# Graph attention block: how W1 and W2 are weighed, and where the preparation of W2 and W3 stands in the queues

## The reference

```python
h = relu(layernorm(x))
xl = (h @ W1).reshape(B, N, 4, 128)              # W1: 256 x 512
e = leaky_relu(sum(xl * att_src1)[:, :, None] + sum(xl * att_dst1)[:, None], 0.2)
h1 = elu(softmax(masked(e), axis=1) applied to xl + b1)
xl2 = h1 @ W2                                    # W2: 512 x 256, one head
e2 = the same with att_src2, att_dst2
x = x + (softmax(masked(e2)) applied to xl2 + b2)
h2 = relu(layernorm(x))
x = x + h2 + h2 @ (weights[0] + weights[1]).T + sum of bias rows by label
```

## Time and profile before

| | |
|---|---|
| median of 3 runs | 498.49 us (498.0 to 501.19) |
| profiled execution, its own time | 501.3 us |
| its span | 499.5 us |
| busy: PE, DVE, ACT, POOL | 471.8, 428.5, 399.6, 320.2 us |
| mean granted tensor clock | 0.988 |
| a pair of x from issue to landing, median of 32 | 2.8 us |

### The profile page before, as it was taken

How to read it: one execution, slowest core, us unless ns; L and a number is a source line. 1 busy time by engine, 2 the same in 40 slices (tenths; PEclk the granted TensorE clock), 3 DMA queues, 4 the chain that set the end, 5 groups by cost and what they waited for, 6 DMA issues and landing times. The chain is left out here.

```text
span 499.5 us, 15008 instructions
## 1 busy us (share of the span) xinstructions
PE 471.8 (94%) x3428; PEld 424.6 (85%) x3428; DVE 428.5 (86%) x1885; ACT 399.6 (80%) x1476; POOL 320.2 (64%) x492
## 2 busy tenths in 40 slices
PE   4488999999999999999999999999999999999875
PEld 1367899999999999999999999999999999999853
DVE  7977888888888988898888988898888988888654
ACT  3247988889888988888888988888888888888831
POOL 2435767676666667766766667766766676766631
PEclk9989999999999999999999999999999999999996
DMA  8011111111111111111111111110111111000001
GB/s 233 21 33 34 36 49 39 56 55 43 36 54 54 54 33 53 54 54 30 46 54 54 54 33 53 54 54 27 48 54 54 54 33 53 22 23 25 21 23 42
DMA packets 29146, 23.70 MB, mean 47 GB/s; under 512 B 1976, under 2 KB 28860, under 8 KB 29120
## 3 DMA queue, kind: packets, MB, share of 16 engines
q1 hardware_dynamic: 27328, 21.44, 14.0%
q10 hardware_dynamic: 1792, 1.98, 1.4%
HBM read 14.56 MB, written 8.39 MB: 46 GB/s over the span
## 5 line engine op out<-in xcount | busy, mean ns | idle before, releaser
L444 ACT ACTIVATE L<-L,nmax 128x128 f32<-128x128 f32 x256 | 99.1, 391 | 5.4 <-DVE nmax L746 3.9
L331 POOL TENSOR_TENSOR h_lo<-h,h_hi 128x512 fp32r<-128x512 f32 x64 | 82.0, 1282 | 24.4 <-DVE h2n L704 20.2
L347 POOL TENSOR_TENSOR P<-L,rsum 128x512 f32<-128x512 f32 x64 | 66.6, 1041 | 20.0 <-DVE rsum L752 18.6
L932 PE MATMUL pY<-w_hi,h_hi 128*128 128x258 f32 x256 | 76.3, 298 | 1.4 <-POOL h_lo L331 1.4
L933 PE MATMUL pY<-w_lo,h_hi 128*128 128x258 f32 x256 | 72.7, 284 | 0.0
L934 PE MATMUL pY<-w_hi,h_lo 128*128 128x258 f32 x256 | 72.3, 282 | 0.0
L460 ACT ACTIVATE elu_e<-pA,minus_ones 128x512 f32<-128x512 f32 x64 | 44.0, 688 | 32.0 <-PE pA L920 32.0
L920 PE MATMUL pA<-PT,xl 128*128 128x128 f32 x512 | 67.7, 276 | 0.5 <-ACT PT L452 0.5
L758 DVE SCALAR_TENSOR_TENSOR h<-elu_e,pA 128x512 f32<-128x512 f32 x64 | 44.0, 688 | 22.8 <-ACT elu_e L460 20.0
L920 PEld LDWEIGHTS pA<-PT,xl 128*128 128x128 f32 x512 | 62.2, 192 | 0.7 <-ACT PT L452 0.7
L746 DVE CUSTOM_DVE_ANT_0 L<-pZ,L 128x128 f32<-128x128 f32 x256 | 58.7, 286 | 3.0 <-ACT L L439 2.9
(11 more groups left out here) (154 smaller groups left out, 1584.2 us busy)
## 6 DMA issues: line engine op xcount, KB each, us to landing
x_all<-in_x SPq DMA_DIRECT2D x32, 256.0 KB, 2.8
out<-x_all SPq DMA_DIRECT2D x32, 256.0 KB, 2.2
adj_all<-in_adj SPq DMA_DIRECT2D x32, 128.0 KB, 2.6
x_all<-in_L_gnn_W ACTq DMA_DIRECT2D x2, 512.0 KB, 6.3
rhs<-lhs SPq DMA_DIRECT2D x64, 6.0 KB
rhs<-lhs SPq DMA_DIRECT2D x64, 1.0 KB
x_all<-in_L_gnn_weights ACTq DMA_DIRECT2D x2, 256.0 KB, 7.3
x_all<-in_L_gnn_att_src ACTq DMA_DIRECT2D x1, 128.0 KB, 6.3
```

The source lines that it names most:

```text
L331: pool.tensor_tensor(h1_lo[p][:, :, :].rearrange("p a b -> p (a b)"), h1[p][:, :], h1_hi[p][:, :, :].rearrange("p a b -> p (a b)").bitcast ...
L347: pool.tensor_tensor(P1[p][:, :, :], L1[p][:, :, :], rsum1[p][:, :].unsqueeze(2).broadcast_to([128, H, 128]), ALU.mult).then_inc(s_P1, 1)
L444: last = act.activation(L1[p][:, h, :], L1[p][:, h, :], ACT.Exp, bias=nmax1[p][:, h:h + 1], scale=-1.0, accum_out=sum1[p][:, h:h + 1])
L932: pe.matmul(pY[:, 0:C2], h1_hi[p][:, k, :], w2_hi[:, k, :], start=(k == 0), stop=False)
```

## The change

The multiplication and the reduction are replaced by one fused operation for each sum (eight over 128 elements for a vector of W1, four over 256 for a vector of W2), each with its accumulator read. `weigh_w2_src` moves from slot -1 to slot 0, behind `leaky1`; `weigh_w2_dst` stays in slot 0 but moves behind `layer_norm1` and `residual1`; `sum_w3` moves from slot 0 to slot 1, behind `take_off_excess`; `split_w3` and tensor's `transpose_w3` move to slots 3 and 2. The sync queue issues the second pair of x and adj only when W1 has landed.

```diff
@@ load
                 if after(g, 4):
                     sp.wait_ge(s_n0, g - 2)
                     sp.wait_ge(s_bn1, g - 2)
+                elif g:
+
+                    sp.wait_ge(s_w1dma, 16)
@@ vector
+            def weigh(rows, vector, products, sums, width):
+
+                blocks = vector.shape[1] // width
+                for k in range(rows.shape[1]):
+                    for b in range(blocks):
+                        cols, m = slice(b * width, (b + 1) * width), k * blocks + b
+                        last = dve.tensor_tensor_reduce(products[:, m * width:(m + 1) * width], rows[:, k, cols], vector[:, cols],
+                                                        1.0, 0.0, ALU.mult, ALU.add, sums[:, m:m + 1])
+                return last
@@ weigh_w1_src
-                link(dve.tensor_tensor(w1_att[:, 0, :].rearrange("p (k n) -> p k n", k=KD), w1_f[:, :, :],
-                                       pA[:, :].unsqueeze(1).broadcast_to([128, KD, HF]), ALU.mult))
-                dve.tensor_reduce(w1_scores[:, 0, :], w1_att[:, 0, :].rearrange("p (m f) -> p m f", f=FH), AX.X, ALU.add)
+                weigh(w1_f, pA[:, :], w1_att[:, 0, :], w1_scores[:, 0, :], FH)
@@ weigh_w1_dst
+                link(weigh(w1_f, pZ[:, :], w1_att[:, 1, :], w1_scores[:, 1, :], FH))
@@ weigh_w2_src
+                weigh(w2_f, att2_bc[:, 0, :], w2_att[:, 0, :], w2_scores[:, 0, :], D)
@@ weigh_w2_dst
+                link(weigh(w2_f, att2_bc[:, 1, :], w2_att[:, 1, :], w2_scores[:, 1, :], D))
@@ the vector list
-            (features1, 1), (sum_w3, 0), (recip1, 1), ... (weigh_w2_dst, 0), (count1, 0), ... (stats1, -4), (weigh_w2_src, -1), (weigh_w1_src, -2), ... (leaky1, 0), (release2, 4), (layer_norm1, -2), (residual1, 4), (label_terms, 3), (take_off_excess, 1), (split_w3, 0), (low_h2, 5), ...
+            (features1, 1), (recip1, 1), ... (count1, 0), ... (stats1, -4), (weigh_w1_src, -2), ... (leaky1, 0), (weigh_w2_src, 0), (release2, 4), (layer_norm1, -2), (residual1, 4), (weigh_w2_dst, 0), (label_terms, 3), (take_off_excess, 1), (sum_w3, 1), (split_w3, 3), (low_h2, 5), ...
@@ the tensor list
-            ... (transpose_h, -1), (transpose_w3, 0), (attend1, 2), ...
+            ... (transpose_h, -1), (transpose_w3, 2), (attend1, 2), ...
```

More of the change, by code:

```diff
@@ L572, in weigh_w1_dst @@
                 dve.wait_ge(s_spread, 2)
-                link(dve.tensor_tensor(w1_att[:, 1, :].rearrange("p (k n) -> p k n", k=KD), w1_f[:, :, :],
-                                       pZ[:, :].unsqueeze(1).broadcast_to([128, KD, HF]), ALU.mult))
-                link(dve.tensor_reduce(w1_scores[:, 1, :], w1_att[:, 1, :].rearrange("p (m f) -> p m f", f=FH), AX.X, ALU.add))
+                link(weigh(w1_f, pZ[:, :], w1_att[:, 1, :], w1_scores[:, 1, :], FH))
                 cols = w1_scores[:, :, :].rearrange("p j (k h) -> p k j h", k=KD)
@@ L589, in weigh_w2_src @@
                 dve.wait_ge(s_w2dma, 64)
-                link(dve.tensor_tensor(w2_att[:, 0, :].rearrange("p (k n) -> p k n", k=KH), w2_f[:, :, :],
-                                       att2_bc[:, 0, :].unsqueeze(1).broadcast_to([128, KH, D]), ALU.mult))
-                dve.tensor_reduce(w2_scores[:, 0, :], w2_att[:, 0, :].rearrange("p (k n) -> p k n", k=KH), AX.X, ALU.add)
+                weigh(w2_f, att2_bc[:, 0, :], w2_att[:, 0, :], w2_scores[:, 0, :], D)
             def weigh_w2_dst(g, p):
@@ L596, in weigh_w2_dst @@
                     return
-                link(dve.tensor_tensor(w2_att[:, 1, :].rearrange("p (k n) -> p k n", k=KH), w2_f[:, :, :],
-                                       att2_bc[:, 1, :].unsqueeze(1).broadcast_to([128, KH, D]), ALU.mult))
-                link(dve.tensor_reduce(w2_scores[:, 1, :], w2_att[:, 1, :].rearrange("p (k n) -> p k n", k=KH), AX.X, ALU.add))
+                link(weigh(w2_f, att2_bc[:, 1, :], w2_att[:, 1, :], w2_scores[:, 1, :], D))
                 scores = w2_scores[:, :, :].rearrange("p j k -> p k j")
@@ L806, in residual2 @@
                 dve.tensor_tensor(of_graph(x_all, g, D), pF[:, 0:D], of_graph(x_all, g, D), ALU.add).then_inc(s_out, 1)
-            pipeline(dve, [(features1, 1), (sum_w3, 0), (recip1, 1), (low_h, -1), (largest_labels, 6), (largest_of_rows, 6), (weigh_w2_dst, 0), (count1, 0), (count2, 3), (elu_max, 2), (recip2, 4), (stats1, -4), (weigh_w2_src, -1), (weigh_w1_src, -2), (layer_norm2, 5), (release1, -4), (low_rows1, -1), (aggregate1, -4), (residual2, 6), (leaky1, 0), (release2, 4), (layer_norm1, -2), (residual1, 4), (label_terms, 3), (take_off_excess, 1), (split_w3, 0), (low_h2, 5), (stats2, 4), (leaky2, 3), (aggregate2, 4), (high_scores2, 2), (weigh_w1_dst, -2), (zero_counts, 2), (low_scores2, 2), (largest_label, 9)])
+            pipeline(dve, [(features1, 1), (recip1, 1), (low_h, -1), (largest_labels, 6), (largest_of_rows, 6), (count1, 0), (count2, 3), (elu_max, 2), (recip2, 4), (stats1, -4), (weigh_w1_src, -2), (layer_norm2, 5), (release1, -4), (low_rows1, -1), (aggregate1, -4), (residual2, 6), (leaky1, 0), (weigh_w2_src, 0), (release2, 4), (layer_norm1, -2), (residual1, 4), (weigh_w2_dst, 0), (label_terms, 3), (take_off_excess, 1), (sum_w3, 1), (split_w3, 3), (low_h2, 5), (stats2, 4), (leaky2, 3), (aggregate2, 4), (high_scores2, 2), (weigh_w1_dst, -2), (zero_counts, 2), (low_scores2, 2), (largest_label, 9)])
             dve.wait_ge(s_label, 1)
@@ L986, in gather_top_label @@
                 pe.matmul(pX[0:1, 0:128], top[:, :], ident[:, :], start=True, stop=True).then_inc(s_toprow, 1)
-            pipeline(pe, [(spread_b1, -1), (transpose_P1, 2), (transpose_h2, 6), (attend2, 5), (sum_w2, 1), (scores2, 4), (project2, 3), (transpose_h, -1), (transpose_w3, 0), (attend1, 2), (transpose_scores2, 3), (scores1, 0), (convolve, 6), (score_terms1, -1), (project1, 0), (transpose_P2, 4), (gather_top_label, 8)])
+            pipeline(pe, [(spread_b1, -1), (transpose_P1, 2), (transpose_h2, 6), (attend2, 5), (sum_w2, 1), (scores2, 4), (project2, 3), (transpose_h, -1), (transpose_w3, 2), (attend1, 2), (transpose_scores2, 3), (scores1, 0), (convolve, 6), (score_terms1, -1), (project1, 0), (transpose_P2, 4), (gather_top_label, 8)])
 _INS = ["x", "adj", "L0_gnn_W1", "L0_gnn_att_src1", "L0_gnn_att_dst1", "L0_gnn_b1", "L0_gnn_W2", "L0_gnn_att_src2",
```

## The result

The changed kernel took 513.74 us (median of 3, 510.03 to 515.69) against 498.49 us: a ratio of 1.027, 95% interval 1.023 to 1.031. It is slower by 13 to 15 us: 13.5 by the ratio, 15.3 by the medians, 14.3 by the two spans. The profiled execution was the slowest of the three (515.69 us); its span is 513.8 us against 499.5.

A forecast was written before the change was run, and what follows sets the result against it. The prediction took the filling of the pipeline as decisive, bound first by the vector engine, then by hand-overs between engines. Terms 0.9 + 1.3 + 1.3 = 3.5, taken as +3.3 on the 498.49 us median, gave 501.8 us, range 498.2 to 505.3.

The forecast's parts named there:

- step 1: Loads in the filling: second pair of x lands at 10.45 us, graph 2's statistics start +2.0 (bounds +0.7 and +5.0).
- step 5: Slot 1: tensor's sums over W2 up to graph 2's transpose take 3.5 us as before; slot 1 starts 0.9 late.
- my two signs of being wrong: In the filling: the second pair lands by 9 us, or the transpose of graph 2 comes before 29.
- step 6: Slots 1 and 2: moved sum_w3 and transpose_w3 delay attend1 and then scalar's exponential, +1.3 (bounds 0.6 and 1.9).
- What bounds the kernel: Tensor sets the steady state; the filling matters, bound by vector to 27.1 us, then by hand-overs between engines.
- Step 2: W1 products: fused operations 0.21 us each, second half's saving lost waiting for gpsimd; low part of h +0.8.
- Step 3: Slot -1 without W2's source half: the low score rows start at 17.5 us, -0.7.
- step 4: Slot 0: first fused minimum at 21.9 us, W2's scores ready at 26.4 against 25.47, +0.9 (bounds +0.9 and +1.6).
- Rival (a): W2 products: fused operations with two SBUF inputs need two cycles an element, +2.1, 503.9 us; chance 0.25.
- rival (b): Tensor idles 3.2 us ahead of L861, which runs at the lower clock: up to 1.7 more, 503.5 us; chance 0.12.
- Step 7: Slot 3: moved split_w3 falls on a busy vector engine, nothing hides it, +1.3.
- Rivals (c) and (d): (c) vector queue sets the pace throughout: 495.7 us, chance 0.12; (d) shift lost in slack before 60 us: 498.5, chance 0.06.

The follow-up runs named there:

- number 7: Kernel before with the fused operations alone, plus fifteen useless matmuls in tensor's idle time of slots -2 and -1: 497.97 us, ratio 0.996.
- number 12: Changed kernel with the load at once and useless matmuls in tensor's idle stretches of slots -2 to 1: 504.27 us, ratio 1.009.
- number 2: Changed kernel with the second pair of x issued at once again: 506.98 us, ratio 1.013.
- number 1: Changed kernel run once more, unchanged: 512.59 us, ratio 1.027.
- Numbers 8 and 9: 8: kernel before with the late second pair alone, 505.69 us; 9: the same with W3's loads on the sync queue behind the third pair, 503.02 us.
- number 10: Kernel before with W3's preparation alone moved (sum_w3, transpose_w3, split_w3 to slots 1, 2, 3): 505.54 us, ratio 1.010.
- W3 in old places: Changed kernel with sum_w3, transpose_w3 and split_w3 back in slot 0: 509.44 us, ratio 1.021.
- W3 moved, filled: Kernel before with fused operations, tensor's idle time filled, and W3's preparation alone moved to slots 1, 2 and 3: 502.22 us, ratio 1.004.
- Number 5: Changed kernel with eight useless matmuls ahead of tensor's wait for W2's scores: 509.76 us, ratio 1.020.
- number 6: Kernel before with the fused operations alone, load at once and all steps at their old places: 497.39 us, ratio 0.995.
- number 3: Changed kernel with the two weighings of W2 at their old places in slots -1 and 0: 507.04 us, ratio 1.014.

## Why the prediction was wrong, by its own steps

The sign was right, the size was not: +3.3 forecast, +14.3 in the profile, and the range ended at 505.3. Two terms of the sum carry most of it: the landing of the second pair (step 1, +2.0 forecast, +4.9 measured) and tensor's time for the sums over W2 (step 5, taken as unchanged, +3.3 measured). Neither of my two signs of being wrong could have shown it, as both looked to the faster side.

The experiments give the same in other shares. From the kernel before to number 7 the medians fall by 2.2 (fused operations, with tensor's idle time filled), to number 12 they rise by 6.3 (new places), to number 2 by 2.7 (the high clock is gone), to number 1 by 5.6 (late load): together +12.5, all but the first across groups. My sum had 2.0 for the load, 1.5 for the fused operations and the places together, and nothing for the clock. So a third term was too small, that of the places (4.1 instead of 1.5); step 6 below says why.

**What bounds the kernel** held, and so did the path: the statistics, the W1 halves, the scores of W2, the sums over W2, the transpose of graph 2.

**Step 1** failed by 2.9 us. The term of the sum was x's landing: I took the third pair's 3.6 us as the nearest row and the pair's own 6.5 us as the bound. It was the bound. The third pair is issued at 10.3, when W2 and W2's vectors have landed (by 10.1) and b2 and W3 are left; the delayed second pair, issued at 6.55, stands behind the end of W2 and all of the rest, and moves its first packet only at 10.0. The row with a full queue beside it was the nearer one. Numbers 8 and 9 show that it is W3's loads, at least, that hold it back.

**Step 2** had the rate right (0.21 us) and the wait for gpsimd's L383 too, but not the second wait, for the mask that gpsimd has queued behind it (0.5 us). **Step 3** and the path of **step 4** held: 1.68 from the low part of h to the low rows (1.6 forecast), 4.67 from there to the first minimum (4.4). The fused form over 256 elements takes 0.35 (0.34); the mask cost 0.46 where I had put 0 to 0.7. Together these waits made the segment from the statistics to W2's scores 17.0 us instead of 15.9.

**Rival (a)** is refuted: with both inputs in SBUF the fused operation takes 0.35 us for 256 elements. The rule of the Trainium skill (Vector Engine (DVE) Microarchitecture Reference, "Points that are easy to get wrong"), half throughput for two SBUF sources that are not bf16, would make it 0.6, an estimate worked out from the page's rule and the 0.34 of step 4. On this instruction the measurement decides. The trace lists the operation as CUSTOM_DVE_ANT_0, and no run shows whether it is of the kind that the page has in mind.

**Step 5** ("3.5 us, as before") failed by 3.3 us in the profile. It took for granted that the sums would run at the high level. I had the other case as **rival (b)** with a chance of 0.12 and a price of 1.7, for L861 alone. The price was 3.3, since the sixteen small matmuls (L863), whose weight loads fill the time, double as well (1.84 to 3.41). The reason that I gave, the idle time ahead of the sums, is borne out by all profiles but one (number 10); I had its 3.2 us right and its chance too low:

| profile | tensor idle ahead of the sums | first part + second part |
|---|---|---|
| changed; again; load at once; W3 in old places | 3.2 us each | 3.78 + 3.41; 3.68 + 1.84; 3.78 + 3.41; 3.26 + 2.29 |
| before; late load; fused and filled; W3 moved, filled | 0.86; 1.31; 1.30; 1.28 | 2.00 + 1.84; 1.99 + 1.84 in the others |
| W2 in old places; late load and late W3; fused only | 0.16 at most | 2.32, 2.13, 1.89, each + 1.84 |
| gap filled; all places, filled | 0.64; 0.36 | 1.99 + 1.84 |
| W3 moved only | 0.58 | 3.78 + 1.94 |

Number 5 shows that it is cause and not company: the same order and the same data, with the idle time filled; number 12 against number 2 shows it a second time (3.78 + 3.41 to 1.99 + 1.84).

**Step 6** gave the right number, 1.3 (number 10), partly by luck. I took attend1's start at 35.02 as what the order of the work gives. But the clock was low from 30.5 to 33.9 in the kernel before, and this had made the slot 1.4 us longer: in numbers 6 to 9, with the same order and the clock high there, it takes 6.05 us instead of 7.41. With the move it takes 8.68 in all profiles but two, so the move itself costs 2.6. The two are the first profile, where it takes 9.33 (the clock fell at 45.5, after the wait for sum_w3, attend1 took 1.70 us instead of 1.16 and the projection behind it ran partly low), and number 3 with 9.79. And sum_w3 took 1.6 us instead of 1.3, beside gpsimd's L373. **Step 7** was right: 1.4 between the marks (1.2 to 1.3 in numbers 10 to 12). Behind it the clock fell once more, at 62.6, and made the next slot 1.5 longer than in the kernel before, which no step of mine had; in number 1 it is 0.1.

So the sum, in the profiled execution: load 4.9, from there to W2's scores 0 (at the old places the fused form gains 2.9, 17.0 to 14.1 in number 6), clock in the sums 3.3, slot 1 another 0.3, slot with transpose_w3 1.9, the next 0.3, slot with split_w3 1.4, the clock behind it 1.5, the rest of the span 0.7: 14.3. This is the account of one execution; that of number 1 has 1.7 less in the sums, 0.6 less in slot 2 and 1.4 less behind split_w3. **Rivals (c) and (d)**, faster and no change, are refuted by the time.

Left open: why the level came late with hardly any idle time (number 10), and why it holds after the sums in one kernel (number 8) and falls in another (before). The runs show that it differs between programs and between executions of one; they do not show a rule. That the 510 to 516 us of the changed kernel spread by it is likely from the two profiles and the correlation in number 1, but not tested. Open too is what holds back the first packet of the late pair.

## What to carry to other kernels

Work that is moved off one engine's path also changes how continuously the others work: look at what the tensor engine did right before each piece of work on the path, and price that piece at both levels of the clock. A load that is delayed is priced by what will be queued and in flight at its issue, not by the nearest transfer of its size. And before a row is taken as a baseline, look at which level of the clock it ran. And a step of the preparation that gives another engine its order (here the scores of W2) goes as early as its data allow; of this change only the fused operations brought time, 0.5%.

## What the runs showed of the hardware that I had not expected

Eight useless matmuls (2.8 us of tensor time) made the kernel 2.8 us faster by the medians, across groups; 1.6 us of it stand at the sums in the profiles. Small matmuls of one column that are bound by their weight loads take 0.115 us each at the high and 0.21 at the low level (1.84 and 3.41 us for sixteen), so the clock holds for weight loads too. A 256 KB load issued while the other queue was full moved its first packet 3.4 to 4.6 us after its issue (six profiles), where the third pair of the kernel before took 1.0. And the same program takes up to 2.6 us more or less in its last 45 us, by how long the clock is low there. A fused vector product whose inputs both lie in SBUF, issued 0.08 us behind the start of a gpsimd subtraction of 2.18 us, took 2.38 us, and its fellow 0.41: it ended 0.28 us after the subtraction, so it waited for all of it. The eight over one SBUF and one PSUM input that ran beside gpsimd's L386 took 0.28 each.
